# A rebuilt ramp in a quantised attention and FFN block: loads in order of need, and four multiplies moved to GpSimd

## The reference

```python
x = x + xattn(layernorm(x), ctx)          # 16 heads of 64
x = x + ffn(layernorm(x))

# xattn: the mask lets query i see the keys j with j % 2048 == i
mask = j_idx % n_q == i_idx               # n_kv = 154, n_q = 2048
sim = where(mask, q @ k.T * scale, -max)
out = softmax(sim) @ v ; return out @ Wout + bout

# ffn
h = layernorm(x) * gamma + beta
h = gelu(qlinear(h, w1, b1)) ; return qlinear(h, w2, b2)
# qlinear: rows of x to int8 by 127 / max|row|, w to {-1, 0, 1} by 1 / mean|w|
```

## Time and profile before

| | |
|---|---|
| median of 3 runs | 547.36 us |
| profiled execution, its time | 546.68 us |
| its span | 545.0 us |
| mean granted TensorE clock | 0.994 |
| TensorE, VectorE, ScalarE, GpSimd busy | 522.7, 451.2, 438.9, 404.7 us |

### The profile page before, as it was taken

The page is one execution under the profiler, slowest core; times in us unless marked ns, Lnnn a source line. Parts: engine busy times, 40 slices in busy tenths (PEclk is TensorE's granted clock), DMA queues, the critical chain, the costliest instruction groups (busy, mean ns, idle before and its releaser), DMA issues.

```text
span 545.0 us, 8050 instructions
## 1 busy us (share of the span) xinstructions
PE 522.7 (96%) x2371; PEld 224.9 (41%) x2418; DVE 451.2 (83%) x762; ACT 438.9 (81%) x444; POOL 404.7 (74%) x532
## 2 busy tenths in 40 slices
PE   6979887999999999999999999999999999999997
PEld 2433333444444444444444444444444444444443
...
GB/s 285 397 395 227 90 43 156 114 232 179 137 140 128 121 127 134 129 141 140 133 126 125 120 141 139 126 123 121 122 139 132 140 141 102 99 67 102 101 78 97
DMA packets 136870, 78.88 MB, mean 145 GB/s; under 512 B 114037, under 2 KB 114037, under 8 KB 136827
## 3 DMA queue, kind: packets, MB, share of 16 engines
...
...
## 4 chain that ended last, share of the span: by engine, by line
PE 75%; issue 2%; ACT 2%; DMA 1%; SPq 1%; DVE 1%; POOL 0%; ACTq 0%; DVEq 0%; POOLq 0%
PE py L1028 37%; PE p L1013 36%; PE p L1003 3%; DMA hT<-hq 1%; DMA out<-xr 1%; ACT hid L541 1%; SPq L220 1%; ACT hq L550 0%; ACT hqT L559 0%; DVE xr L818 0%; SPq L228 0%; ACT xq L532 0%; DVE hmax L795 0%; DVE hid L789 0%; DVE xmax L777 0%
## 5 line engine op out<-in xcount | busy, mean ns | idle before, releaser
L1028 PE MATMUL py<-w2q,hqT 128*128 128x512 bf16 x1006 | 230.0, 379 | 3.8 <-DVE w2q L759 2.8
L1013 PE MATMUL p<-w1q,xqT 128*128 128x512 bf16 x995 | 229.0, 380 | 2.5 <-issue 1.4
L541 ACT ACTIVATE hid<-p,xdeq 128x1024 f32<-128x1024 f32 x128 | 141.7, 1108 | 26.8 <-PE p L1013 16.4
L550 ACT ACTIVATE hq<-hid,hscale 128x2048 int8<-128x2048 f32 x64 | 128.1, 2001 | 38.7 <-DVE hscale L801 38.7
L1028 PEld LDWEIGHTS py<-w2q,hqT 128*128 128x128 bf16 x1024 | 100.1, 98 | 123.9 <-issue 3.3
L1013 PEld LDWEIGHTS p<-w1q,xqT 128*128 128x128 bf16 x1024 | 95.0, 98 | 120.6 <-issue 14.9
L350 POOL TENSOR_TENSOR hx<-hx,beta_b 128x512 f32<-128x512 f32 x64 | 92.6, 1467 | 11.4 <-ACT hx L526 11.4
L795 DVE TENSOR_REDUCE hmax<-hid 128x1 f32<-128x1025 f32 x64 | 78.1, 1220 | 21.7 <-ACT hid L541 21.3
L335 POOL TENSOR_TENSOR xr<-xr,attn 128x512 f32<-128x512 f32 x64 | 81.8, 1295 | 18.0 <-DVE attn L691 13.3
L354 POOL TENSOR_TENSOR xr<-xr,b_b 128x512 f32<-128x512 f32 x64 | 92.4, 1462 | 0.0
L789 DVE TENSOR_REDUCE hid<-hid 128x1 f32<-128x1024 f32 x64 | 77.4, 1210 | 8.9 <-ACT hid L541 8.9
...
## 6 DMA issues: line engine op xcount, KB each, us to landing
...
```

The costliest lines, as they stand in the source:

```text
L541: nc.scalar.activation(hid[:, t % 2, h * HALF:(h + 1) * HALF], p1[:, h * HALF:(h + 1) * HALF], ACT.Gelu, scale=col(xdeq, t)).then_inc(gelu ...
L550: nc.scalar.activation(hq8[:, t % 2, :], hid[:, t % 2, 0:HID], ACT.Copy, scale=col(hscale, t))\
L1013: mm = nc.tensor.matmul(p1[:, n * D:(n + 1) * D], xT[:, k, :], w1q[:, k, n * D:(n + 1) * D], start=False, stop=(k == KD - 1))
L1028: mm = nc.tensor.matmul(py[:, t % 2, :], hqT[:, t % 2, c // 2, c % 2, :], w2q[:, c, :], start=(c == 0), stop=(c == 2 * NJ - 1))
```

## The change

The change rewrites the ramp's lists and some of what they call; the loop from s = 6 is the same text.

- *Loads.* b1 is loaded once into 16 partitions instead of four times over 32. All w2 pieces, x0, bout, gamma and beta move from ScalarE's queue to SP's, w2 behind w1, the context and tiles 0 to 5. ScalarE's queue has only wout. w2 pieces 0 to 4 use other buffers, so x12 to x15 wait for roundings of w2 inside `load_x`.
- *b1.* GpSimd splits it into three pieces on 16 partitions; SP stores them to device memory and reads them back into 12 rows at each of four partition offsets of `b1rows`, which GpSimd clears first. VectorE's `bias_rows` and the two affine selects go.
- *The table.* ScalarE begins with a gelu of two columns.
- *TensorE.* Eight fp32 matmuls of 128 columns run first. The products run for column blocks 0 and 1 over all chunks, then blocks 2 and 3; `weight_total(0)` comes behind all of them, both first `out_rows` ahead of `bias(0)`, and `tail_product` behind tile 2. The second layer of tile 0 is in two halves.
- *1/std.* For tiles 2 to 5 GpSimd multiplies, by a new `times_std` of its own.

Functions, changed lines only:

```diff
+            def load_w2(j):
+                if j == 3:
+                    sp.wait_ge(mean_done, 1)
+                if j == 5:
+                    sp.wait_ge(wvo_done, KD)
+                sp.dma_start(w2raw[j], w2T[j * 2 * P:(j + 1) * 2 * P, :].rearrange("(p e) n -> p e n", e=2))\
+                    .then_inc(w2_loaded[j], 16)
...
+                elif t >= 12:
+                    sp.wait_ge(wround_act[1], 1 if t < 14 else 4)
...
+            def store_b1():
+                sp.wait_ge(b1_split, 5)
+                sp.dma_start(b1_pieces.rearrange("b a (p n) -> p (b a) n", n=P), b1p.rearrange("p b a n -> p (b a) n")).then_inc(b1_stored, 16)
+
+            def load_b1_rows():
+                sp.wait_ge(const_set, 4)
+                sp.wait_ge(b1_stored, 16)
...
+            def times_std(t):
+                pool.wait_ge(rstd_ready, t + 1)
+                pool.wait_ge(xgamma_done, t + 1)
+                pool.tensor_scalar(htile(t)[:, 0, :], htile(t)[:, 0, :], col(rstd, t), 1.0, ALU.mult, ALU.mult).then_inc(xstd_pool, 1)
...
-                pool.wait_ge(xstd_done, t + n)
+                if 2 <= t <= 5:
+                    pool.wait_ge(xstd_pool, t - 1)
+                else:
+                    pool.wait_ge(xstd_done, t + n - (4 if t > 5 else 0))
...
+            def first_gelu():
+                act.wait_ge(const_set, 2)
+                nc.scalar.activation(wpart[:, 0, 6:8], neg_half[:, :], ACT.Gelu).then_inc(vmean_done, 1)
...
+            def warm_up():
+                pe.wait_ge(const_set, 1)
+                for _ in range(8):
+                    nc.tensor.matmul(pa[:, 0:P], ones[:, :], ones[:, :], start=True, stop=True)
...
-                    m, k = i // KD, i % KD
-                    if k == 0:
+                    m, k = (i // 2, i % 2) if i < 2 * KI else (i % KI, i // KI)
+                    if i < 2 * KI and k == 0:
...
-                    pe.wait_ge(wq_ready[1], 8)
+                    pe.wait_ge(wq_ready[1], last // 2)
```

More of the change, by code:

```diff
@@ L31, with block_program @@
 QMAX = 127.0
-def block_program(nc, x, ctxm_d, ctxt_d, wvT, wout_d, bout, w1T, b1, w2T, b2, gamma, beta, ctx_b0, out, tail_rows):
+def block_program(nc, x, ctxm_d, ctxt_d, wvT, wout_d, bout, w1T, b1, w2T, b2, gamma, beta, ctx_b0, out, tail_rows, b1_pieces):
     es = ExitStack()
@@ L629, in _ @@
             gelu(4, 0)
-            times_std(9)
+            round_h(3)
             gelu(4, 1)
-            round_h(3)
-            widen_h(2)
             round_x(6)
             round_x(7)
-            round_h(4)
+            widen_h(2)
+            times_std(8)
             gelu(5, 0)
@@ L639, in _ @@
             widen_h(3)
+            round_h(4)
+            times_std(9)
             times_std(10)
@@ L848, in _ @@
             statistics(1)
-            abs_w1(4)
-            centre(1)
             statistics(2)
             statistics(3)
-            weight_sum(0)
-            x_scale(0, 1)
-            weight_scale(0)
+            centre(1)
             centre(2)
             centre(3)
+            abs_w1(4)
+            x_scale(0, 1)
+            x_scale(1, 1)
+            statistics(4)
+            weight_sum(0)
             ctx_sum(0)
             ctx_sum(1)
-            x_scale(1, 1)
+            weight_scale(0)
+            centre(4)
+            ctx_sum(2)
+            ctx_sum(3)
+            statistics(5)
             round_w1(0)
@@ L881, in _ @@
             weight_scale(1)
+            statistics(6)
+            statistics(7)
+            attn_rows(1)
+            hidden_scale(0)
+            ctx_means()
+            half_scale(1)
+            hidden_scale(1)
+            x_scale(4, 2)
+            statistics(8)
+            statistics(9)
+            half_scale(2)
+            hidden_scale(2)
+            centre(6)
             centre(7)
-            hidden_scale(0)
-            x_scale(4, 2)
             tail_rows_out()
-            statistics(8)
-            half_scale(1)
-            statistics(9)
-            hidden_scale(1)
-            statistics(10)
-            centre(8)
-            centre(9)
-            half_scale(2)
-            statistics(11)
-            centre(10)
-            centre(11)
-            hidden_scale(2)
+            attn_rows(2)
+            centre(8)
+            widen_h(0)
+            clip(1, 0)
             clip(1, 1)
+            clip(1, 2)
+            clip(1, 3)
+            clip(1, 4)
             clip(1, 5)
-            clip(1, 0)
             clip(1, 6)
-            clip(1, 3)
-            widen_h(0)
-            clip(1, 2)
+            widen_h(1)
             clip(1, 7)
-            clip(1, 4)
-            widen_h(1)
-            attn_rows(1)
-            attn_rows(2)
             half_scale(3)
@@ L915, in _ @@
             half_scale(4)
+            statistics(11)
+            centre(9)
+            widen_h(2)
+            widen_h(3)
             hidden_scale(4)
-            widen_h(2)
+            centre(10)
+            half_scale(5)
+            centre(11)
+            hidden_scale(5)
             result(1)
             x_scale(8, 2)
-            widen_h(3)
-            half_scale(5)
-            hidden_scale(5)
             for s in range(6, T + LAG + 1):
@@ L1015, in first_layer, with second_layer @@
                 mm.then_inc(ffn1_done, 1)
-            def second_layer(t):
+            def second_layer(t, first=0, last=2 * NJ):
                 pe.wait_ge(hcast_dve, t + 1)
@@ L1026, in second_layer @@
                     pe.wait_ge(y_ready, t - 1)
-                for c in range(2 * NJ):
+                for c in range(first, last):
                     mm = nc.tensor.matmul(py[:, t % 2, :], hqT[:, t % 2, c // 2, c % 2, :], w2q[:, c, :],
                                           start=(c == 0), stop=(c == 2 * NJ - 1))
-                mm.then_inc(ffn2_done, 1)
+                if last == 2 * NJ:
+                    mm.then_inc(ffn2_done, 1)
+            warm_up()
             context_mean()
```

311 lines of the change are left out of this document (150 added, 161 removed).

## The result

The changed kernel took 549.86 us (median of 20 runs, 546.47 to 553.03), the kernel before 548.35 us (20 runs on the same chip). The ratio is 1.0039, with a 95% interval of 1.0023 to 1.0055: slower by 0.4%, where 541.3 us and faster had been forecast. The profiled execution took 550.42 us, its span 548.6.

What follows compares the result with a forecast made beforehand. TensorE was taken as the bound, busy 522.7 of 545.0 us, with savings only ahead of tile 6's bias at 105.1 us. Terms: 10.6 - 2.6 - 1.9 = 6.1 us, so 547.36 - 6.1 = 541.3 us; range 537.0 to 545.6.

Steps and rivals of the forecast that it cites:

- Mark 1: Mean-row matmul, where TensorE restarts its products: from 24.71 to 23.9 us, gain 0.8.
- the clock falls: TensorE's 2 us wait for the mean row lowers its clock; 14 passes cost 3.2 more; 544.5 us; chance 0.12.
- Mark 2: End of TensorE's products: from 47.0 to 39.6 us, gain 7.4, without the idle 2.98 and slow-clock 3.2.
- Mark 3: End of the second layer of tile 0: from 92.5 to 81.9 us, gain 10.6 in all.
- GpSimd's multiply: Four 1/std multiplies moved from ScalarE to GpSimd in the ramp, taken at 0.8 us each, bounds 0.61 and 1.39.
- covered: GpSimd's longer list still lands the transposes of tiles 0 and 2 before need, by 2.4 us for tile 2.
- GpSimd pays more: Multiply at 1.39 us and stretched VectorE instructions cost 0.5 of cover and 1.0 to 1.4; 543.0 us; chance 0.10.
- Mark 4: From second_layer(0)'s end to the bias of tile 6: VectorE's result(0) waits for GpSimd's hidden_deq(0); loss 2.6 us.
- Mark 5: Into the steady part: VectorE lags about 3 us, so bias(7) and bias(8) wait 0.5 and 1.4; loss 1.9 us.
- The rival on the slower side: Steady loop: handovers lock into a wait in each tile; 0.25 us a tile costs 14.5, 549.7 us; chance 0.08.
- the early part is not early: w1 or the chunks land as before, and later weight_total(0) delays w1's scale; 546.5 us; chance 0.05.
- the first rival: VectorE's wait for hidden_deq(0) doesn't bite because work behind it has slack; gain 10.6, 536.8 us; chance 0.20.

Runs made afterwards that it cites:

- e10: Changed kernel with four order edits; in tiles 2 to 5 VectorE's first-half hidden-row maximum is taken over 64 columns only: 546.34 us, ratio 0.9984.
- e1: Changed kernel with w2 pieces 5 to 7 and x tiles 6 to 8 issued ahead of tile 0's transpose on SyncE: 546.86 us, ratio 0.9975.
- e4: Changed kernel with the 1/std multiply of tiles 2 to 5 back on ScalarE: 547.15 us, ratio 0.9991.
- e7: Kernel before the change, with only the 1/std multiply of tiles 2 to 5 moved to GpSimd: 550.44 us, ratio 1.0048.
- e2: Changed kernel with GpSimd's hidden_deq(0) and (1) behind widen_x(4, 2) instead of widen_x(6, 2): 548.59 us, ratio 1.0015.
- e6: Changed kernel with unused filler matmuls, 20 ahead of weight_total(1) and 12 ahead of second_layer(2): 548.57 us, ratio 1.0015.
- e5: Changed kernel with store(0) and store(1) together ahead of load_x(16) in SyncE's list: 548.57 us, ratio 1.0013.
- e9: Changed kernel: w2 pieces 5, 6 before tile 0's transpose, early hidden_deq, 1/std on ScalarE, stores paired, times_std(9) before widen_h(3), round_h(4): 545.74 us, ratio 0.998.
- e11: e9 with the transposes of tiles 8 and 9 ahead of load_x(17) and spread_tail(2) in SyncE's list: 545.15 us, ratio 0.9949.
- e12: e11 with GpSimd's scale_rows(8, 2) ahead of add_beta(10) and add_beta(11): 545.3 us, ratio 0.9965.

## Why the prediction was wrong

*Mark 1* (mean row, forecast 23.9) measured 23.03: right, a little better. The wait there is 1.81 us and the clock stays 1.00, so the rival *the clock falls* didn't come at this place. It came behind two waits that no rival had, 5.44 and 3.04, and cost 1.45 and 1.69 there. Nor was it far here: in e10 the gap was 2.02, and the 36 passes behind it took 17.14 us instead of 15.61.

*Mark 2* (products through, forecast 39.6) measured 38.5: right, and by its mechanism.

*Mark 3* (end of the second layer of tile 0, forecast 81.9, gain 10.6) measured 89.39, gain 3.1. **This is the step that failed.** From the products' end to this mark the forecast has 38.3 us of work and 4 of idle; measured are 9.4 of waits and 0.6 of start, 1.45 for the lower clock and 39.4 of work. The term that failed is GpSimd's multiply, put at nothing because it was "covered". The step walked VectorE, ScalarE and GpSimd, but not SyncE's list, though w2's pieces 5 to 7 stand in it behind a transpose that waits for GpSimd. e1 moves the pieces: 4.6 of the 5.44 us go, 1.9 come back as a longer wait at bias 0, and the mark comes at 86.40. e4 takes the multiplies away: 3.0 of the 5.44 and the 1.56 at bias 0 go, and the mark comes at 83.45, within 1.6 us of the forecast.

*GpSimd's multiply.* Its own length was right: 0.83 us on average, taken at 0.8, in bounds of 0.61 to 1.39:
```profile
L399 POOL TENSOR_SCALAR hx<-hx,rstd 128x512 f32<-128x512 f32 x4 | 3.3, 830 | 0.0
```
"Covered" was wrong. The cover was reckoned from the transposes of tiles 0 and 2 to their bias matmuls alone; that of tile 2 held, that of tile 0 landed at 48.03 where the forecast said 46.5, 1.56 after the need, and the w2 pieces behind it have no cover at all. e4 and e7, one from each side, put the price of the multiply at about 0.5% (1.0039 to 0.9991, and 1.0048 alone), some 2.6 us (in e7 by another path, so that the sizes agree proves no common cause); the forecast had 0, and 1.5 to 1.9 in the rival *GpSimd pays more*. That rival had the culprit, but not the path. The port part was seen from one side only, as longer VectorE instructions, and for those with two SBUF inputs, the centres; here VectorE's centres were no longer than before (960 ns on average against 1112), and it was GpSimd's 128x1 subtractions that took 1.05 and 1.11 instead of 0.19. They began at 42.31 and 43.44 and ended at 43.36 and 44.55; VectorE's two roundings of w1, which have one tensor input, took 1.25 and 1.27 and ended at 43.31 and 44.50. In one line:
```profile
42.06 2.45 DVE L774 TENSOR_SCALAR w1q<-raw,wscale 128x2048 int16<-128x2048 f32 x2
```
Each small instruction ended 0.05 us behind one rounding. The Trainium skill (SBUF — State Buffer, section "SBUF: two separate sides") says that the port pair which the two engines share is an exclusive lock: of a GpSimd instruction and a VectorE instruction in a two-port mode or with two SBUF inputs, whichever starts first has it for its whole length. By this, if the roundings are in such a mode, a small instruction costs what is left of the large one beside it, and the trace agrees with 1.05 and 1.11. That they are in one no row says; they go through 2048 columns in 1.25 us, where a VectorE reduction takes 1.21 for 1024.

*Mark 4* (loss 2.6 at the bias of tile 6) measured 4.7: the wait was right, the size not. VectorE waited for hidden_deq(0):
```profile
97.50 0.75 DVE L843 SCALAR_TENSOR_TENSOR xr<-py,hdeq,xr 128x512 f32<-128x512 f32 x1 [4.46 <-POOL hdeq L444]
```
TensorE's part in it is 3.04, my walk's 3.0; the other 1.69 are the lower clock behind the gap (5.31 for 3.62), which the term had not priced. e2 removes both, e6 the clock's part alone. That part looks like chance: in e5 the clock stayed at 1.00 behind the same 3.04, and the stretch lost 3.0.

*Mark 5* (loss 1.9 by tile 8) measured 2.1, as a wait for tile 8's transpose. The lag that the forecast named was there, but it came to TensorE through GpSimd. VectorE's `hidden_scale(4)` stands behind its wait of 4.46; ScalarE waits 3.04 for it, with `times_std(9)` next in its list; GpSimd waits 2.90 for that, and tile 8's widening stands behind. ScalarE, GpSimd (two lines), SyncE:
```profile
103.59 2.00 ACT L596 ACTIVATE hq<-hid,hscale 128x2048 int8<-128x2048 f32 x1 [3.04 <-DVE hscale L826]
```
```profile
106.28 1.27 POOL L409 TENSOR_TENSOR hx<-hx,beta_b 128x512 f32<-128x512 f32 x1 [2.90 <-ACT hx L572]
...
117.35 1.04 POOL L440 CAST xq<-xq 128x1024 bf16<-128x1024 int16 x1
```
```profile
118.94 2.54 SPq L253 DMA_TRANSPOSE xqT<-xq  x2
```
The widening ends at 118.39, so SyncE's own order of issues cost at most 0.55 us in the changed kernel. This chain is read from the trace; e2, which takes VectorE's wait away, has the widening end 1.6 us earlier (116.81). e5 excludes the order of the stores, e10 VectorE's amount of work. Only where GpSimd is earlier does SyncE's order count: in e9 the widening ended at 109.58 and the transpose left at 112.39, behind load_x(17) and the tail's three copies; e11 puts it ahead of them, and bias 8 came 2.0 us earlier. The wait at tile 8 also takes back much of what an edit wins before it: in e1, e2, e4 bias 6 moved by 4.7, 3.5 and 6.3 us, bias 8 by 2.1, 1.7 and 3.4.

*The sum.* Forecast 10.6 - 2.6 - 1.9 = +6.1; measured 3.1 - 4.7 - 2.1 = -3.7 in the profiled execution. Of the 9.8 us between them 7.5 are mark 3, 2.1 mark 4 and 0.2 mark 5. The rival on the slower side, a slower steady part, did not come about: the pace is 7.35 in both. What would have shown the forecast wrong, by its last part, was a second layer of tile 0 ending after 87; it ended at 89.4.

Some of the prediction's numbers don't follow, though none moves its forecast. Between 47.8 and 92.5 us the kernel before has a third wait of 1.54 us, at the bias of tile 3, which is no smaller than the 1.42 shown. 10.6 MB at 400 GB/s are 26.5 us; the 30.5 has 4 us in it that are not named. The slower steady part at 0.25 us a tile gives 541.3 + 14.5 = 555.8, not 549.7, and the rival *the early part is not early* 541.3 + 6 = 547.3, not 546.5. The 536.8 of the first rival lies just outside the range that was to hold it.

Open is whether a version with the orders of e9, e11 and e12 and the multiply still on GpSimd would do as well (not tried), what decides whether the clock falls behind a gap of some 3 us, and the spread of single executions, 543 to 548 us in e11, which the two profiles of a pair cannot resolve.
